# Row statistics for the next stage's normalisation, taken at the end of each stage

## The chip, the cores and the metric

The kernel runs on one core of one Trainium2 chip. The metric is the device time of one execution in microseconds. Three executions of the kernel before took 2994.44, 2995.75 and 3001.46 us, so the median is 2995.75 us.

## What is computed

The input `x` is 1024 tokens of 512 numbers. Two layers of blocks work on it. Each block normalises the rows (mean and variance over the 512 numbers of a token), computes something from the normalised rows and adds the result to `x`:

```python
def _layernorm(x, axis=-1, eps=1e-05):
    m = jnp.mean(x, axis=axis, keepdims=True)
    v = jnp.var(x, axis=axis, keepdims=True)
    return (x - m) / jnp.sqrt(v + eps)
# the pattern of every block: x = x + block(_layernorm(x))
```

The blocks, in the order in which the kernel runs them, are: attention with 32 heads of 16 (stage L0a), an expert choice of one in four with low-rank weights (L0f), attention with one head of 128 (L0b), the low-rank block again (L0g), attention with 32 heads of 128 (L1a), a routed block with 16 experts of which each token takes four (L1f), attention with heads of 16 again (L1b), and the routed block again (L1g).

## The kernel before

`x` stays in SBUF for the whole run, as `g.x`: eight tiles (`NT = 8`) of 128 tokens by 512 numbers in f32. The run is a row of stages: `constants` (it loads `x` and builds a few masks), the eight blocks above, and `store`. Every stage allocates its own semaphores and its own SBUF tiles, and ends with a barrier of all engines (line 73). No instruction of a stage, and none of its DMAs, is issued before the stage ahead of it has passed that barrier. So the loads of a stage's weights start when the stage starts.

Each engine works off its own list in order. Waits name a semaphore and a value.

At the start of each block stage VectorE (DVE) runs `ln_stats` (line 111): eight `bn_stats`, one for each tile of `x` (line 114), eight `bn_aggr` (line 117), one addition of the epsilon for all tiles (line 119), then a wait for ScalarE (ACT), which takes one square root for all tiles in `ln_root` (line 127), and a reciprocal (line 121). Then `ln_row` (line 133) writes the normalised tiles one by one, two ahead, and TensorE (PE) turns each by four transposes (`ln_turn`, line 141).

What stands between the first rows and the first products differs from stage to stage:

- `attention16` (L0a, L1b): DVE and PE wait for six loads (`w_loaded` at 96) after two rows.
- `lora_ffn` (L0f, L0g): PE turns one row, then waits for three loads (`loaded` at 48); DVE waits for the same three after two rows. The last of the three is `ebias`. The first product behind them is line 808.
- `single_head` (L0b): DVE waits for five loads (`loaded` at 80) straight behind the statistics and ahead of the first row, for line 1011; PE waits for the same five ahead of everything. The last one is `bo`.
- `attention128` (L1a): DVE waits for four loads (`loaded` at 64) after two rows, for line 1441. The last one is `bo`.
- `routed_ffn` (L1f, L1g): DVE waits for two small loads (`loaded` at 32) after two rows, for lines 1876 and 1878; the last one is `gb`. Then row 2 is written, and `xl` of row 0 (line 1059) starts a loop in which PE, ACT and DVE hand each row on.

Each stage ends with additions of the block's result into the tiles of `g.x` on DVE: line 740 (`attention16`), 855 (`lora_ffn`), 1028 (`single_head`), 1472 (`attention128`) and 2028 (`routed_ffn`, where both summands come back from HBM by DMA). In `attention128` the order of the last steps on DVE is written out by hand: the additions of the last head come in the order of tiles 0, 1, 3, 2, 4, 5, 6, 7, with work on the probabilities (line 1456, tile `pl`) between them, and PE's last large product waits for the last `pl`.

Of the kernel before, what the change touches and what calls it, by code (L numbers as in the profile page):

```python
# [14 lines left out]
P = 128  # L15
# [60 lines left out]
class Shared:  # L76


    def __init__(self, nc, ctx):
# [8 lines left out]
        self.sum_dram = [nc.dram_tensor(f"sum{i}", (T + P, H), F32, kind="Internal").ap() for i in range(3)]  # L88
        self.padded = nc.alloc_semaphore("padded")
# [8 lines left out]

class Normalisation:


    def __init__(self, sb, sem, depth=2):
        self.depth = depth
        self.xn = sb("xn", [P, depth, H])
        self.stats, self.mv = sb("stats", [P, NT, 6]), sb("mv", [P, NT, 2])
        self.veps, self.std, self.rstd = sb("veps", [P, NT]), sb("std", [P, NT]), sb("rstd", [P, NT])
        self.step, self.std_ready = sem("ln_step"), sem("std_ready")
        self.row_ready, self.turned = sem("row_ready"), sem("row_turned")


def ln_stats(dve, g, n):

    for t in range(NT):
        dve.bn_stats(n.stats[:, t, :], g.x[:, t, :]).then_inc(n.step, 1)
    for t in range(NT):
        dve.wait_ge(n.step, NT)
        dve.bn_aggr(n.mv[:, t, :], n.stats[:, t, :]).then_inc(n.step, 1)
    dve.wait_ge(n.step, 2 * NT)
    dve.tensor_scalar_add(n.veps[:, :], n.mv[:, :, 1], EPS).then_inc(n.step, 1)
    dve.wait_ge(n.std_ready, 1)  # L120
    dve.reciprocal(n.rstd[:, :], n.std[:, :]).then_inc(n.step, 1)
    dve.wait_ge(n.step, 2 * NT + 2)


def ln_root(act, n):
    act.wait_ge(n.step, 2 * NT + 1)
    act.activation(n.std[:, :], n.veps[:, :], ACT.Sqrt).then_inc(n.std_ready, 1)


def ln_row(dve, g, n, t):  # L130
    if t >= n.depth:
        dve.wait_ge(n.turned, t - n.depth + 1)
    dve.tensor_scalar(n.xn[:, t % n.depth, :], g.x[:, t, :], n.mv[:, t, 0:1], n.rstd[:, t:t + 1],
                      ALU.subtract, ALU.mult).then_inc(n.row_ready, 1)
# [23 lines left out]
def constants(nc, g, d):  # L158
    with stage(nc, "const") as (sb, sem):
        done = sem("done")  # L160
        loaded = sem("loaded")
        with nc.Block() as block:
            @block.sync
            def _(sp):
                sp.dma_start(g.x[:, :, :], d["x"]).then_inc(loaded, 16)
                sp.wait_ge(loaded, 16)

# [140 lines left out]
def attention16(nc, g, d, name, first):  # L308
    with stage(nc, name) as (sb, sem):
        ln = Normalisation(sb, sem)  # L310
# [3 lines left out]
        with nc.Block() as block:  # L314
# [69 lines left out]
            def _(act):  # L384
# [31 lines left out]
                ln_root(act, ln)  # L416
# [41 lines left out]

# [286 lines left out]
def lora_ffn(nc, g, d, name):  # L745

    with stage(nc, name) as (sb, sem):
        ln = Normalisation(sb, sem)
# [17 lines left out]
        with nc.Block() as block:  # L766
# [17 lines left out]
            def _(act):  # L784
                ln_root(act, ln)
                for t in range(NT + 2):
# [3 lines left out]
                    if t >= 2:  # L790
# [3 lines left out]
                        act.activation(zT[:, t % 2, :], g.bank(3)[:, 0:P], ACT.Copy).then_inc(zT_ready, 1)  # L794

# [32 lines left out]
            def _(dve):  # L828
                ln_stats(dve, g, ln)
                ln_row(dve, g, ln, 0)  # L830
                ln_row(dve, g, ln, 1)
                dve.wait_ge(filled, NE0 + 2)
                dve.wait_ge(loaded, 48)
                for t in range(NT + 2):
# [18 lines left out]
                    if t >= 2:  # L853
                        dve.wait_ge(out_ready, t - 1)
                        dve.tensor_tensor(g.x[:, t - 2, :], g.bank((t - 2) % 3), g.x[:, t - 2, :], ALU.add)\
                            .then_inc(added, 1)

def single_head(nc, g, d, name):  # L860
    with stage(nc, name) as (sb, sem):
        ln = Normalisation(sb, sem)
# [20 lines left out]
        with nc.Block() as block:  # L883
# [13 lines left out]
            def _(act):  # L897
                ln_root(act, ln)
# [36 lines left out]
                ctx_copy(NT - 1)  # L935

# [71 lines left out]
            def _(dve):  # L1008
                ln_stats(dve, g, ln)
                dve.wait_ge(loaded, 80)  # L1010
                dve.tensor_scalar(bqs[:, :], bq[:, 0:1], -SCALE, None, ALU.mult).then_inc(bias_ready, 1)
                for t in range(NT):
                    ln_row(dve, g, ln, t)
                for t in range(NT):
# [18 lines left out]
                for qt in range(NT):  # L1033
# [7 lines left out]
                    if qt >= 2:  # L1041
                        add(qt - 2)
                add(NT - 2)
                add(NT - 1)

# [108 lines left out]
ROPES = list(LIN)  # L1154

# [41 lines left out]
def attention128(nc, g, d, name):  # L1197
    with stage(nc, name) as (sb, sem):
        ln = Normalisation(sb, sem)
# [48 lines left out]
        with nc.Block() as block:  # L1248
# [44 lines left out]
            def _(act):  # L1293
                ln_root(act, ln)
# [3 lines left out]
                for s in ACT_STEPS:  # L1298
# [36 lines left out]
                    else:  # L1335
# [13 lines left out]
                        mm.then_inc(lin_ready, 1)  # L1349

# [85 lines left out]
            def _(dve):  # L1436
                ln_stats(dve, g, ln)
# [702 lines left out]
```

## Time and profile before

| | |
|---|---|
| median of three executions | 2995.75 us |
| the profiled execution, its own time | 2997.02 us |
| its span in the profile | 2995.0 us |
| PE busy | 2652.2 us, 89% of the span |
| DVE busy | 1907.5 us, 64% |
| ACT busy | 1514.3 us, 51% |
| POOL busy | 822.2 us, 27% |
| mean granted TensorE clock | 0.945 of 2.4 GHz |

The profile lists, engine by engine, each instruction with its line, the tile that it writes, the tiles that it reads, its start and its duration. A timeline line reads: start in us from the span's start, duration in us, engine, line, operation, out<-in, the shape, and how many instructions of that kind are merged into it. What stands in brackets is the time that the engine had been idle before it, and what ended that. Busy time is no proof of a bound: what bounds a stretch is read from which wait ended last there.

### The profile page before, as it was taken

Reading aid. Unit: us, or ns where it says so; the run is one execution under the profiler, and the core shown is the slowest. Engines: PE = TensorE matmul, PEld = TensorE weight load, DVE = VectorE, ACT = ScalarE, POOL = GpSimd, SP = SyncE. Lnnn points to the kernel's source line nnn. Section 1 sums busy time; section 2 is a strip of 40 time slices with the busy share of each in tenths; the row PEclk is TensorE's granted clock in tenths of the full one; section 3 lists DMA queues with packets and bytes.
Section 4 is the critical chain, followed back from the end, with each engine's and each line's share of the span. In section 5 each row is a group of like instructions: output and inputs, shape, how many; then the busy total and the mean of one; then the engine's idle time right before and its main releaser. Section 6 shows DMA issues by size and latency. Waiting matters only on the chain. (4 is left out here: it accounts for less than half of the span.)

```text
span 2995.0 us, 46427 instructions
## 1 busy us (share of the span) xinstructions
PE 2652.2 (89%) x14824; PEld 1793.2 (60%) x14886; DVE 1907.5 (64%) x3382; ACT 1514.3 (51%) x2540; POOL 822.2 (27%) x777
## 2 busy tenths in 40 slices
PE   6789988886999999999999987999578888778995
PEld 4444434454888888888888864666344444345663
DVE  5666642444777787777777766677556666166774
ACT  4466661222555555555555541566265666324663
POOL 1200000104343443445335301455120000003552
PEclk9799998997999999999999988999788999979998
DMA  2100000001000000000000023988500000029887
GB/s 76 71 1 0 0 1 16 19 17 46 19 22 22 22 22 18 22 22 26 15 22 25 8 92 135 297 201 199 144 1 1 0 0 0 11 107 322 211 201 197
DMA packets 68154, 196.92 MB, mean 66 GB/s; under 512 B 9040, under 2 KB 9936, under 8 KB 62608
## 3 DMA queue, kind: packets, MB, share of 16 engines
q1 hardware_dynamic: 46928, 145.44, 14.2%
q0 software_dynamic: 21056, 49.30, 8.7%
q8 instruction: 96, 1.57, 0.2%
q14 instruction: 74, 0.61, 0.1%
HBM read 154.33 MB, written 40.37 MB: 65 GB/s over the span
## 5 line engine op out<-in xcount | busy, mean ns | idle before, releaser
L1315 ACT ACTIVATE L1a_ph<-single 128x512 fp32r<-128x512 f32 (+3 forms) x384 | 174.2, 489 | 180.4 <-PE single L1402 179.7
L698 DVE TENSOR_REDUCE L1b_least<-single 128x1 f32<-128x512 f32 (+3 forms) x304 | 191.2, 660 | 107.9 <-PE single L520 75.9
L698 DVE TENSOR_REDUCE L0a_least<-single 128x1 f32<-128x512 f32 (+3 forms) x304 | 191.1, 660 | 106.9 <-PE single L520 75.5
L1456 DVE TENSOR_TENSOR L1a_pl<-single,L1a_ph 128x512 fp32r<-128x512 f32 (+3 forms) x384 | 199.5, 549 | 52.7 <-ACT L1a_ph L1315 52.0
L1472 DVE SCALAR_TENSOR_TENSOR x<-single,L1a_rinv,x 128x512 f32<-128x512 f32 x256 | 189.5, 745 | 58.4 <-PE single L1066 58.4
L1306 ACT ACTIVATE L1a_probs<-pair,L1a_least 128x128 f32<-128x128 f32 (+7 forms) x256 | 190.0, 744 | 72.0 <-DVE L1a_least L1450 70.8
L1450 DVE TENSOR_REDUCE L1a_least<-pair 128x1 f32<-128x128 f32 (+7 forms) x256 | 190.8, 750 | 43.3 <-PE pair L1391 42.6
L1283 POOL TENSOR_TENSOR L1a_swapped<-L1a_swapped,L1a_sin 128x512 f32<-128x512 f32 x80 | 129.8, 1622 | 303.7 <-ACT L1a_swapped L1347 303.7
L409 ACT ACTIVATE L1b_probsT<-pair 128x896 f32<-128x896 f32 (+2 forms) x192 | 151.2, 811 | 67.4 <-PE pair L539 48.1
L409 ACT ACTIVATE L0a_probsT<-pair 128x896 f32<-128x896 f32 (+2 forms) x192 | 151.2, 811 | 65.9 <-PE pair L539 46.5
L1402 PE MATMUL single<-ident,L1a_probs 128*128 128x128 f32 x1152 | 169.0, 274 | 1.4 <-ACT L1a_probs L1306 1.4
L1064 PE MATMUL single<-L1a_xh,L1a_wh 128*128 128x512 f32 x384 | 160.4, 418 | 6.0 <-POOL L1a_wl L1272 4.6
L1066 PE MATMUL single<-L1a_xh,L1a_wl 128*128 128x512 f32 x384 | 152.6, 397 | 0.0
L1065 PE MATMUL single<-L1a_xl,L1a_wh 128*128 128x512 f32 x384 | 152.6, 397 | 0.0
L1289 POOL TENSOR_TENSOR L1a_ql<-L1a_lin,L1a_qh 128x512 fp32r<-128x512 f32 x64 | 85.6, 1337 | 234.9 <-DVE L1a_qh L1494 234.9
L1888 DVE TENSOR_TENSOR L1g_wl<-L1g_store,L1g_wh 128x1024 fp32r<-128x1024 f32 x94 | 111.2, 1222 | 60.3 <-ACT L1g_wh L1704 59.2
L1888 DVE TENSOR_TENSOR L1f_wl<-L1f_store,L1f_wh 128x1024 fp32r<-128x1024 f32 x94 | 111.2, 1223 | 59.9 <-ACT L1f_wh L1704 58.9
L1064 PE MATMUL pair<-L1a_kh,L1a_qh 128*128 128x512 f32 (+3 forms) x384 | 141.0, 367 | 6.9 <-POOL L1a_ql L1289 5.5
L1402 PEld LDWEIGHTS single<-ident,L1a_probs 128*128 128x128 f32 x1152 | 130.0, 141 | 13.2 <-ACT L1a_probs L1306 1.7
L516 PE MATMUL single<-L1b_qkT 96*128 (+3 forms) x384 | 122.6, 356 | 13.0 <-DVE L1b_least L698 8.5
L1065 PE MATMUL pair<-L1a_kl,L1a_qh 128*128 128x512 f32 (+3 forms) x384 | 133.1, 347 | 0.0
L1066 PE MATMUL pair<-L1a_kh,L1a_ql 128*128 128x512 f32 (+3 forms) x384 | 133.1, 347 | 0.0
(517 smaller groups left out, 7052.1 us busy)
## 6 DMA issues: line engine op xcount, KB each, us to landing
L1f_wd<-in_L1f_w SPq DMA_DIRECT2D x48, 512.0 KB, 4.3
L1g_wd<-in_L1f_w SPq DMA_DIRECT2D x48, 512.0 KB, 4.2
L1a_raw<-in_L1a_w SPq DMA_DIRECT2D x80, 256.0 KB, 2.6
L1f_store<-in_L1f_w SPq DMA_DIRECT2D x16, 1024.0 KB, 7.9
L1g_store<-in_L1f_w SPq DMA_DIRECT2D x16, 1024.0 KB, 8.4
sum<-L0a_pad_row SPq DMA_DIRECT2D x2, 2304.0 KB, 11.7
sum<-x SPq DMA_DIRECT2D x16, 256.0 KB, 2.9
x<-sum SPq DMA_DIRECT2D x16, 256.0 KB, 4.7
```

What stands on the lines that cost most here:

```text
L409: act.activation(a.probsT[:, i % 2, j, 0:n], g.pair[u % 2][:, 0:n], ACT.Exp, scale=-1.0)\
L698: dve.tensor_reduce(a.least[:, part, qt, first:first + heads], g.bank(4 + f % 2)[:, 0:heads * w].rearrange("p (j k) -> p j k", j=heads), A ...
L1064: pe.matmul(out, wh, xh, start=start, stop=False)
L1065: pe.matmul(out, wh, xl, start=False, stop=False)
L1066: return pe.matmul(out, wl, xh, start=False, stop=stop)
L1306: act.activation(probs[:, u % 2, 0:n], g.pair[u % 2][:, 0:n], ACT.Exp, bias=least[:, u % 4:u % 4 + 1], scale=-1.0, accum_out=rsum[:, h % 2 ...
L1315: act.activation(p_tile(ph, u, i), turned_bank(u, i), ACT.Copy).then_inc(p_high, 1)
L1402: mm = pe.transpose(g.bank(4 + b % 2)[:, k * P:(k + 1) * P], probs[:, u % 2, kt * P:(kt + 1) * P], g.ident[:, :])
L1450: dve.tensor_reduce(least[:, u % 4:u % 4 + 1], g.pair[u % 2][:, 0:(u % NT + 1) * P], AX_X, ALU.min)\
L1456: dve.tensor_tensor(p_tile(pl, u, i), turned_bank(u, i), p_tile(ph, u, i).bitcast(F32), ALU.subtract)\
L1472: dve.scalar_tensor_tensor(out=g.x[:, t, :], in0=aux_bank(("O", h, t)), scalar=rinv[:, h % 2, t:t + 1], in1=g.x[:, t, :], op0=ALU.mult, op ...
L1888: dve.tensor_tensor(wl[:, s, :, :], src, wh[:, s, :, :].bitcast(F32), ALU.subtract).then_inc(w_split, 1)
```

## The change

Each stage now takes the statistics of the stage behind it, and no stage but `constants` takes its own. Two sets of small tiles (`Moments`) live for the whole run, and each stage swaps them.

- For each tile of `x`, `ln_next` waits for the addition into that tile (or, in `constants`, for the load of `x`), then issues three instructions on DVE, each waiting for the one before: `bn_stats`, `bn_aggr`, and the addition of the epsilon for this tile alone. A call for a tile stands behind the addition into the next tile; the calls for the last two tiles stand behind the last addition (in `single_head` the last three calls are spread over the last two additions).
- ACT takes the square root of the first seven tiles in one instruction (`ln_next_root`) when their values are there; DVE takes one reciprocal of them at the very end (`ln_next_scale`).
- The next stage has only the eighth tile's root (`ln_last_root`, ACT, at its start) and reciprocal (`ln_last_scale`, DVE, behind the first two rows) left; `ln_row` of the eighth tile waits for it.
- `ln_stats` and its calls at the start of the eight block stages are gone. The last block stage, L1g, takes no statistics for a stage behind it.
- Each stage has two more semaphores.

```diff
-def ln_stats(dve, g, n):
-
-    for t in range(NT):
-        dve.bn_stats(n.stats[:, t, :], g.x[:, t, :]).then_inc(n.step, 1)
-    for t in range(NT):
-        dve.wait_ge(n.step, NT)
-        dve.bn_aggr(n.mv[:, t, :], n.stats[:, t, :]).then_inc(n.step, 1)
-    dve.wait_ge(n.step, 2 * NT)
-    dve.tensor_scalar_add(n.veps[:, :], n.mv[:, :, 1], EPS).then_inc(n.step, 1)
...
+LATE = NT - 1
+LAST = "L1g"
+
+
+def ln_last_root(act, n):
+
+    act.activation(n.now.std[:, LATE:NT], n.now.veps[:, LATE:NT], ACT.Sqrt).then_inc(n.std_ready, 1)
+
+
+def ln_last_scale(dve, n):
+
     dve.wait_ge(n.std_ready, 1)
...
+    dve.reciprocal(n.now.rstd[:, LATE:NT], n.now.std[:, LATE:NT]).then_inc(n.step, 1)
+
+
+def ln_next(dve, g, n, t, added, count, turn=None):
+
+    m, turn = n.after, t if turn is None else turn
+    dve.wait_ge(added, count)
+    dve.bn_stats(m.stats[:, t, :], g.x[:, t, :]).then_inc(n.next_step, 1)
+    dve.wait_ge(n.next_step, 3 * turn + 1)
+    dve.bn_aggr(m.mv[:, t, :], m.stats[:, t, :]).then_inc(n.next_step, 1)
+    dve.wait_ge(n.next_step, 3 * turn + 2)
+    dve.tensor_scalar_add(m.veps[:, t:t + 1], m.mv[:, t, 1:2], EPS).then_inc(n.next_step, 1)
+
+
+def ln_next_root(act, n):
+
+    act.wait_ge(n.next_step, 3 * LATE)
+    act.activation(n.after.std[:, 0:LATE], n.after.veps[:, 0:LATE], ACT.Sqrt).then_inc(n.next_std_ready, 1)
+
+
+def ln_next_scale(dve, n):
+
+    dve.wait_ge(n.next_std_ready, 1)
+    dve.reciprocal(n.after.rstd[:, 0:LATE], n.after.std[:, 0:LATE]).then_inc(n.next_step, 1)
...
+            @block.vector
+            def _(dve):
+                for t in range(NT):
+                    ln_next(dve, g, ln, t, loaded, 16)
+                ln_next_scale(dve, ln)
...
             @block.vector
             def _(dve):
-                ln_stats(dve, g, ln)
                 ln_row(dve, g, ln, 0)
                 ln_row(dve, g, ln, 1)
+                ln_last_scale(dve, ln)
                 dve.wait_ge(a.w_loaded, 96)
...
                     dve.tensor_tensor(g.x[:, t, :], g.bank(t % 2), g.x[:, t, :], ALU.add).then_inc(a.added, 1)
+                    if t >= 1:
+                        ln_next(dve, g, ln, t - 1, a.added, t)
+                ln_next(dve, g, ln, NT - 1, a.added, NT)
+                ln_next_scale(dve, ln)
...
+                        turn = LAST_ADDED.index(t) if h == HEADS128 - 1 else 0
+                        if turn >= 1:
+                            before = LAST_ADDED[turn - 1]
+                            ln_next(dve, g, ln, before, added, ADDED["o", h, before], turn - 1)
...
                     dve.wait_ge(back_loaded[t], 32)
                     dve.tensor_tensor(g.x[:, t, :], other[:, t, :], g.x[:, t, :], ALU.add).then_inc(back, 1)
+                    if name != LAST and t >= 1:
+                        ln_next(dve, g, ln, t - 1, back, t)
+                if name != LAST:
+                    ln_next(dve, g, ln, NT - 1, back, NT)
+                    ln_next_scale(dve, ln)
```

## Rows read from the trace of the kernel before

**Rows 1.** Timeline, from the end of L0a to L0f's first product.

```profile
484.94 0.69 DVE L740 TENSOR_TENSOR x<-pair,x 128x512 f32<-128x512 f32 x1 [3.75 <-PE pair L624]
...
486.55 1.28 ACT L127 ACT_TABLE_LOAD   x1 [5.41 <-PEq L73]
486.59 4.84 DVE L114 BATCH_NORM_STATS2 L0f_stats<-x 128x6 f32<-128x512 f32 x8 [0.96 <-PEq L73]
...
487.42 0.42 SPq L771 DMA_DIRECT2D L0f_ebias<-in_L0f_bias  x1
...
491.47 0.64 DVE L117 BATCH_NORM_AGGREGATE L0f_mv<-L0f_stats 128x2 f32<-128x6 f32 x8
...
492.83 1.00 DVE L133 TENSOR_SCALAR L0f_xn<-x,L0f_mv,L0f_rstd 128x512 f32<-128x512 f32 x2
493.43 1.97 PE L141 MATMUL single<-ident,L0f_xn 128*128 128x128 f32 x8 [8.53 <-DVE L0f_xn L133]
...
495.23 1.93 PE L808 MATMUL single<-L0f_ga,L0f_xT 128*128 128x36 f32 x8
```

**Rows 2.** Tiles x and L0f_mv: count, ns min/median/max, first and last start, shape.

```profile
L114 DVE BATCH_NORM_STATS2 L0f_stats<-x x8: 675/676/695, 486.6 to 490.8; 128x6 f32<-128x512 f32 x8
...
L117 DVE BATCH_NORM_AGGREGATE L0f_mv<-L0f_stats x8: 147/148/182, 491.5 to 492.0; 128x2 f32<-128x6 f32 x8
...
L119 DVE TENSOR_SCALAR L0f_veps<-L0f_mv x1: 172/172/172, 492.1 to 492.1; 128x8 f32<-128x8 f32 x1
```

**Rows 3.** DMA issues: transfer, queue, count, KB each, us from issue to landing.

```profile
L0b_bo<-in_L0b_bo SPq DMA_DIRECT2D x1, 256.0 KB, 4.5
...
L0f_ebias<-in_L0f_bias SPq DMA_DIRECT2D x1, 2.0 KB, 4.8
...
L0g_ebias<-in_L0f_bias SPq DMA_DIRECT2D x1, 2.0 KB, 5.4
L1f_gb<-in_L1f_bias SPq DMA_DIRECT2D x1, 8.0 KB, 2.7
```

**Rows 4.** Timeline, what the starts of L0a, L0b and L1a wait for.

```profile
21.34 6.89 PE L468 MATMUL pair<-L0a_w,L0a_xT 128*128 128x512 f32 x16 [3.23 <-DMA L0a_bd<-in_L0a_bd]
...
548.52 0.43 SPq L890 DMA_DIRECT2D L0b_bo<-in_L0b_bo  x1
...
553.10 0.15 DVE L1011 TENSOR_SCALAR L0b_bqs<-L0b_bq 128x1 f32<-128x1 f32 x1
...
700.39 0.18 DVE L1441 TENSOR_SCALAR L1a_bias<-L1a_bias 128x32 f32<-128x32 f32 x1 [0.39 <-DMA L1a_bo<-in_L1a_bo]
```

**Rows 5.** Timeline, the start of L1f (L1g repeats it).

```profile
1766.38 0.43 SPq L1596 DMA_DIRECT2D L1f_gb<-in_L1f_bias  x1
...
1773.20 0.18 DVE L1876 CAST L1f_gwh<-L1f_gw 128x64 fp32r<-128x64 f32 x1
...
1774.66 0.69 DVE L1059 TENSOR_TENSOR L1f_xl<-single,L1f_xh 128x512 fp32r<-128x512 f32 x1 [0.56 <-ACT L1f_xh L1052]
```

**Rows 6.** Timeline, DVE in the middle of L0b.

```profile
610.19 1.23 DVE L1020 TENSOR_REDUCE L0b_least<-pair 128x1 f32<-128x1024 f32 x1 [0.91 <-PE pair L964]
```

**Rows 7.** Timeline, DVE at the end of L1a.

```profile
1753.04 1.29 DVE L1456 TENSOR_TENSOR L1a_pl<-single,L1a_ph 128x512 fp32r<-128x512 f32 x2 [0.41 <-ACT L1a_ph L1315]
...
1761.75 1.44 DVE L1472 SCALAR_TENSOR_TENSOR x<-single,L1a_rinv,x 128x512 f32<-128x512 f32 x2 [1.14 <-PE single L1066]
...
1763.64 1.45 DVE L1472 SCALAR_TENSOR_TENSOR x<-single,L1a_rinv,x 128x512 f32<-128x512 f32 x2 [0.45 <-PE single L1066]
```

**Rows 8.** Timeline, the second and the last of L1f's eight closing additions.

```profile
2124.16 0.69 DVE L2028 TENSOR_TENSOR x<-L1f_store,x 128x512 f32<-128x512 f32 x1 [1.36 <-DMA L1f_store<-sum]
...
2132.32 0.69 DVE L2028 TENSOR_TENSOR x<-L1f_store,x 128x512 f32<-128x512 f32 x1 [0.59 <-DMA L1f_store<-sum]
```

**Rows 9.** Stretches: us, busy PE PEld DVE ACT POOL, PEclk, DMA share, GB/s.

```profile
488.00:489.00 1.00, 0.00 (x0) 0.00 (x0) 1.00 (x3) 0.00 (x0) 0.00 (x0) 0.76 0.98 166
...
502.00:503.00 1.00, 1.00 (x3) 0.33 (x2) 0.00 (x0) 0.00 (x0) 0.00 (x0) 0.91 0.00 0
```

More of the change, by code:

```diff
@@ L88, in __init__ @@
         self.sum_dram = [nc.dram_tensor(f"sum{i}", (T + P, H), F32, kind="Internal").ap() for i in range(3)]
+        self.moments = tuple(Moments(sb, n) for n in range(2))
         self.padded = nc.alloc_semaphore("padded")
@@ L95, in bank, with __init__ @@
         return self.pair[i // 2][:, (i % 2) * HALF:(i % 2 + 1) * HALF] if i < 4 else self.single[i - 4][:, :]
+class Moments:
+    def __init__(self, sb, n):
+        self.stats, self.mv = sb(f"stats{n}", [P, NT, 6]), sb(f"mv{n}", [P, NT, 2])
+        self.veps, self.std, self.rstd = sb(f"veps{n}", [P, NT]), sb(f"std{n}", [P, NT]), sb(f"rstd{n}", [P, NT])
 class Normalisation:
-    def __init__(self, sb, sem, depth=2):
+    def __init__(self, sb, sem, g, depth=2):
         self.depth = depth
         self.xn = sb("xn", [P, depth, H])
-        self.stats, self.mv = sb("stats", [P, NT, 6]), sb("mv", [P, NT, 2])
-        self.veps, self.std, self.rstd = sb("veps", [P, NT]), sb("std", [P, NT]), sb("rstd", [P, NT])
+        self.now, self.after = g.moments
+        g.moments = (self.after, self.now)
@@ L132, in ln_row @@
         dve.wait_ge(n.turned, t - n.depth + 1)
-    dve.tensor_scalar(n.xn[:, t % n.depth, :], g.x[:, t, :], n.mv[:, t, 0:1], n.rstd[:, t:t + 1],
+    if t == LATE:
+        dve.wait_ge(n.step, 1)
+    dve.tensor_scalar(n.xn[:, t % n.depth, :], g.x[:, t, :], n.now.mv[:, t, 0:1], n.now.rstd[:, t:t + 1],
                       ALU.subtract, ALU.mult).then_inc(n.row_ready, 1)
@@ L856, in _ @@
                             .then_inc(added, 1)
+                    if t >= 3:
+                        ln_next(dve, g, ln, t - 3, added, t - 2)
+                ln_next(dve, g, ln, NT - 1, added, NT)
+                ln_next_scale(dve, ln)
 def single_head(nc, g, d, name):
     with stage(nc, name) as (sb, sem):
-        ln = Normalisation(sb, sem)
+        ln = Normalisation(sb, sem, g)
         xT = sb("xT", [P, KC, T])
@@ L935, in _ @@
                 ctx_copy(NT - 1)
+                ln_next_root(act, ln)
             @block.tensor
@@ L1013, in _ @@
                     ln_row(dve, g, ln, t)
+                    if t == 1:
+                        ln_last_scale(dve, ln)
                 for t in range(NT):
@@ L1042, in _ @@
                         add(qt - 2)
+                    if qt >= 3:
+                        ln_next(dve, g, ln, qt - 3, added, qt - 2)
                 add(NT - 2)
+                ln_next(dve, g, ln, NT - 3, added, NT - 2)
                 add(NT - 1)
+                ln_next(dve, g, ln, NT - 2, added, NT - 1)
+                ln_next(dve, g, ln, NT - 1, added, NT)
+                ln_next_scale(dve, ln)
 def turned_rows_high(act, g, ln, xh, ready):
@@ L1154 @@
 ROPES = list(LIN)
+LAST_ADDED = [s[2] for s in DVE_STEPS if s[0] == "o" and s[1] == HEADS128 - 1]
 def piece_of(step):
@@ L1494, in _ @@
                         dve.tensor_copy(rope_to(kind, of, half, kh, qh), lin[:, r, :]).then_inc(rot_high, 1)
+                ln_next(dve, g, ln, LATE, added, ADDED["o", HEADS128 - 1, LATE])
+                ln_next_scale(dve, ln)
 GU = KC
```

41 lines of the change are left out of this document (23 added, 18 removed).

## The prediction

> **What bounds the kernel now.** I read the timeline around each of the eight stage boundaries, since the change moves work only there, and asked at each which wait ended last. At the end of L0a the last addition starts at 484.94, the barrier lets L0f go at 486.55, DVE takes its statistics, and the first normalised row starts at 492.83 [rows 1]. So 6.24 us lie between the first `bn_stats` (486.59) and the first row, and PE is idle all that time. This is what the change goes for: eight stages times 6.24 is 49.9 us.
>
> The second view is that of the DMA issues: a stage's loads are issued when the stage starts, and some land later than the statistics end. Then the removed time was not on the path. The third is the end of each stage, where the new work goes: is DVE waiting between its additions, or is it the last to finish?
>
> **The price of one tile.** `bn_stats` lasts 0.676 us alone, `bn_aggr` 0.148, the addition of epsilon 0.172 [rows 2]. Each waits for the one before. Such a hand-over took 0.04 us: eight `bn_stats` from 486.59 last 4.84 and end at 491.43, and `bn_aggr` starts at 491.47 [rows 1]. The next instruction, where it does not depend on the last one, starts some 0.08 us before its end: eight times 0.676 would be 5.41, and they took 4.84 [rows 1, 2]. A tile therefore costs 0.676 + 0.04 + 0.148 + 0.04 + 0.172 - 0.08 = 1.0 us on DVE. Before, a tile cost 4.84/8 + 0.64/8 = 0.69, as the small instructions followed each other without waits. Bounds: 0.96 (a 0.04 hand-over is hidden) and 1.12 (no overlap at the end, and one hand-over more).
>
> The Trainium skill (VectorE: DVE Perf Modes, The DRAIN you can't avoid) says that the next operation doesn't start until the pipeline is empty, and that the semaphore costs nothing extra. The 4.84 us above contradict the first half. By the page a tile would cost 1.08 to 1.12, and the sum below would be some 3 us higher.
>
> **What is added at the stage ends.** A call of `ln_next` keeps back whatever stands behind it on DVE.
>
> - Simple tail (L0a, L0f, L0b, L0g, L1b): the earlier tiles lie in DVE's idle time between additions, 3.75 us a tile in L0a [rows 1]. In `lora_ffn` they delay the choice of an expert for the next tile by about 0.6 us, with PE's main product as cover. In L0b the tightest place is the minimum at line 1020, ahead of which DVE idles 0.91 us for PE [rows 6]; 1.0 us goes in there, so 0.1 us could show, and I take nothing. If the cover were gone, each of these tiles would cost its 1.0. Behind the last addition stand two tiles and the reciprocal of about 0.2: 2.2 us, five times, 11.0 us. The barrier then follows as before (485.63 to 486.55, [rows 1]).
> - `constants`: eight tiles and the reciprocal behind the load of `x`, and nothing to hide them: 8 x 1.0 + 0.2 = 8.2 us. The weights of L0a are issued only behind the barrier, so they are late by the same.
> - L1a, ahead of PE's last large product: two tiles come before the last `pl` (line 1456), ahead of which DVE idled 0.41 us [rows 7]. 2.0 - 0.4 = 1.6 us. Bounds 0 (other idle time absorbs it) and 2.0.
> - L1a, behind it: four additions and now five tiles. The additions ran from 1761.75 to 1763.64 + 1.45 = 1765.09 [rows 7]. After: 4 x 0.70 + 5 x 1.0 + 0.2 = 8.0, that is to 1769.75. Cost 4.7 us. PE's last two products wait for additions in this queue, but DVE is later than they are anyway.
> - L1f: the closing additions follow the loads, one each 1.36 us, the last seven from 2124.16 to 2132.32 + 0.69 = 2133.01 [rows 8]. With a tile of 1.0 behind each addition of 0.61, DVE needs 1.6 a tile and becomes the bound: 7 x 0.61 + 8 x 1.0 + 0.2 = 12.5, to 2136.6. Cost 3.6 us. L1g takes no statistics: 0.
>
> Sum of costs: 11.0 + 8.2 + 1.6 + 4.7 + 3.6 = 29.1 us. The square root of seven tiles runs on ACT beside the last tile's statistics. That of the eighth, at the stage start, and its reciprocal are needed six rows later. Two more semaphores a stage I take at nothing; the bound above is 0.1 us a stage.
>
> **What is gained at the stage starts.** Times stay those of the old trace, with the stage start held fixed.
>
> - L0a: PE had been idle 3.23 us when the last of six loads landed and let the products start at 21.34 [rows 4]. Gain 0. L1b repeats this (12.3 us from its start to the load): 0.
> - L0b: `bo` is issued at 548.52 and lands 4.5 us later, at 553.02 [rows 3, 4]. DVE's first instruction behind it starts at 553.10 [rows 4], and it stands ahead of the rows. Statistics and load end together: gain at most 0.1. I take 0.
> - L1a: DVE waits for `bo` until 700.39, after 0.39 us of idling [rows 4]. Only the first two rows get earlier. Gain 0.
> - L0f: `ebias` is issued at 487.42 and lands at 492.22 [rows 1, 3]. PE has then to turn row 1, four of the eight transposes that took 1.97 us [rows 1], some 0.9 us, and starts line 808 at 493.2. Before: 495.23 [rows 1]. Gain 2.1, bounds 1.1 and 3.0 (two turnings or none).
> - L0g: the same, but `ebias` lands 0.6 us later [rows 3]: gain 1.5.
> - L1f: `gb` lands at 1766.38 + 2.7 = 1769.08 [rows 3, 5]. Lines 1876 and 1878 and row 2 then took from 1773.20 to 1774.10, where DVE began to wait for ACT [rows 5]: 0.9 us. So line 1059 starts at 1770.0 instead of 1774.66 [rows 5]. Gain 4.6. What follows is a chain of hand-overs that moves as a whole. L1g: `gb` lands 0.2 later in its stage, gain 4.5.
>
> Sum of gains: 2.1 + 1.5 + 4.6 + 4.5 = 12.7 us. Net: 29.1 - 12.7 = 16.4 us slower. The profiled execution took 2997.02 us (span 2995.0 and 2.0 around it), so it would take 3013.4; the median of the runs is 1.3 us lower, which gives 3012.1 us, 0.55% more. A measurement of this kernel can tell about 0.3% (9 us) from no change.
>
> **Rivals.**
>
> - The loads get out of the way (faster). If the loads land earlier once DVE no longer reads `x` while they write, stages held by loads gain too. With no stage held by its loads the gain is 49.9 - 29.1 = 20.8 us: 2975 us. It turns the sign once the loads land some 2 us earlier in each of the eight stages. For it: loads and statistics do overlap, with the DMA engines busy for 0.98 of the stretch from 488 to 489 [rows 9]. Against it: in L0a DVE had nothing to do for the last microseconds, and the loads still landed 3.23 us after PE had run dry [rows 4]. Chance 0.04.
> - The clock stays up (no change). The granted clock fell between 488 and 489, some 3.6 us after PE's last product, and rose between 502 and 503 [rows 9], 8.7 us after PE's first transposes at 493.43 [rows 1]. At half speed that loses at most 4.3 us. If the shorter pause held the clock at 2.4 GHz in L0f, L0g, L1f and L1g, up to 17 us would come back: 2995 us. Against it: PE's first transpose would start at 485.63 + 2.2 + 0.92 + 0.64 = 489.4, still behind the fall, and PE then stops again for the load. Chance 0.05. The Trainium skill (TensorE: Matmul & The Clock Gate, Why this matters for your kernels) advises to avoid pauses of PE for this reason; by it shorter pauses speak for this change, and by it the time would be this rival's 2995.
> - Dearer hand-overs (slower still). Some 32 tiles lie on the path (8 + 10 + 7 + 8, less what idle time covers). If a tile costs 1.5 us instead of 1.0, that adds 16 us: 3028 us. Against it: the 0.04 us measured. Chance 0.05.
> - The square root comes late. At the ends of five stages (L0a, L0b, L1a, L1f, L1b) ACT changes its table; L0f and L0g have it already. If the 1.28 us of the load [rows 1] started only when the seventh tile's values are there, root and load take 1.5 against the 1.0 of the last tile: 0.5 us each, 3015 us in all, within the range. Against it: the load at 486.55 ran ahead of its wait [rows 1]. Chance 0.06. The Trainium skill (ScalarE: Activation LUTs, What ACT_TABLE_LOAD costs) puts a switch at 2.66 us, with a drain; by that it would be some 1.9 us a stage, near 3020.
>
> **How the numbers follow.** The forecast of 3012 us has a chance of 0.80. Its own range: the price of a tile moves it by -1 to +4, the middle of L1a by -1.6 to +0.4, the starts of L0f and L0g by 1 each way, the moment at which the clock rises after each boundary by some 3 in all (L0f's 8.7 us is one draw), the median of three runs by 2. Together that is 3006 to 3018, and with the late root and part of the clock's rival 3005 to 3019. Faster by over 0.3%: 0.04. Within 0.3%: 0.10, from the clock and from the case that several tails are half hidden. Slower by over 0.3%: 0.86.
>
> **What would show it.** In the new profile: L0a's products start some 8 us later than 21.34. From the last addition's end to the next stage's first instruction it is 3.1 us in the simple tails against 0.9. L0b's line 1011 and L1a's line 1441 stand as far from their stage's start as before, with some 6 to 8 us of idle DVE ahead. L1f's line 1059 starts 4.6 us nearer to its stage's start. The closing additions of L1f come 1.6 us apart. The prediction is wrong if the loads of L0b, L1a, L0a or L1b land earlier in their stages, or if a tile costs much other than 1.0 us.

## The result, and the profile after

The changed kernel took 3011.77 us, the median of 13 executions (3008.34 to 3016.97). Beside them 13 executions of the kernel before had a median of 3001.46 us (2993.57 to 3005.6). The ratio is 1.0041, with a 95% interval of 1.003 to 1.0053: slower by 12.3 us, 9 to 16 (the ratio on record is not that of the two medians, which are 10.3 us apart). A second comparison, told below, gave 1.0049 (1.003 to 1.0067). So the change costs about 0.4 to 0.5%.

| | before | after |
|---|---|---|
| profiled execution | 2997.02 us | 3011.77 us |
| its span | 2995.0 us | 3009.7 us |
| PE busy | 2652.2 us | 2660.0 us |
| DVE busy | 1907.5 us | 1923.2 us |
| mean granted clock | 0.945 | 0.946 |

What follows are timelines of the changed kernel, in the columns told with the profile of before. A call of the new `ln_next` is three lines: L140 (`bn_stats`), L142 (`bn_aggr`), L144 (epsilon). The first and the last call of `constants`, with the reciprocal, and PE's first products in L0a (they answer to the first line of [rows 4]):

```profile
8.64 0.69 DVE L140 BATCH_NORM_STATS2 stats<-x 128x6 f32<-128x512 f32 x1 [8.64 <-DMA x<-in_x]
9.37 0.18 DVE L142 BATCH_NORM_AGGREGATE mv<-stats 128x2 f32<-128x6 f32 x1
9.59 0.15 DVE L144 TENSOR_SCALAR veps<-mv 128x1 f32<-128x1 f32 x1
...
15.69 0.68 DVE L140 BATCH_NORM_STATS2 stats<-x 128x6 f32<-128x512 f32 x1
...
16.69 0.19 DVE L156 RECIPROCAL rstd<-std 128x7 f32<-128x7 f32 x1
```

```profile
29.65 1.22 PE L510 MATMUL pair<-L0a_w,L0a_xT 128*128 128x512 f32 x1 [7.82 <-DMA L0a_bd<-in_L0a_bd]
```

Eight calls take from 8.64 to 16.69, so 1.006 us each. The products start 8.31 us later than at 21.34, and PE idles 7.82 us for the same load `bd` where it idled 3.23: the shorter start only makes the wait for the load longer.

DVE from L0a's last addition to L0f's first row, and PE to L0f's first product (they answer to [rows 1]):

```profile
495.98 0.69 DVE L782 TENSOR_TENSOR x<-pair,x 128x512 f32<-128x512 f32 x1 [2.75 <-PE pair L666]
496.59 0.68 DVE L140 BATCH_NORM_STATS2 stats<-x 128x6 f32<-128x512 f32 x1
...
497.59 0.68 DVE L140 BATCH_NORM_STATS2 stats<-x 128x6 f32<-128x512 f32 x1
...
498.60 0.19 DVE L156 RECIPROCAL rstd<-std 128x7 f32<-128x7 f32 x1
499.77 0.76 DVE L164 TENSOR_SCALAR L0f_xn<-x,mv,rstd 128x512 f32<-128x512 f32 x1 [0.98 <-PEq L73]
```

```profile
505.41 1.11 PE L172 MATMUL single<-ident,L0f_xn 128*128 128x128 f32 x4 [3.71 <-DMA L0f_ebias<-in_L0f_bias]
506.31 0.91 PE L855 MATMUL single<-L0f_ga,L0f_xT 128*128 128x36 f32 x4
```

Two calls and the reciprocal stand behind the last addition. From its start to the first row it is 3.79 us, of which 2.14 are new. From that row to line 855 it is 6.54 us, and PE waits 3.71 of them for `ebias`. From the last addition to the first product it was 10.29 us before and is 10.33 now: tail and gain cancel.

Where L0b and L1a begin, DVE waits for `bo` (the last two lines of [rows 4]):

```profile
566.65 0.15 DVE L1062 TENSOR_SCALAR L0b_bqs<-L0b_bq 128x1 f32<-128x1 f32 x1 [7.37 <-DMA L0b_bo<-in_L0b_bo]
...
716.67 0.18 DVE L1502 TENSOR_SCALAR L1a_bias<-L1a_bias 128x32 f32<-128x32 f32 x1 [8.14 <-DMA L1a_bo<-in_L1a_bo]
```

The end of L1a on DVE (it answers to [rows 7]). First the second of the last head's eight additions before, the one into tile 1:

```profile
1750.16 0.75 DVE L1472 SCALAR_TENSOR_TENSOR x<-single,L1a_rinv,x 128x512 f32<-128x512 f32 x1 [0.39 <-PE single L1066]
```

The same after, from the second of the last head's eight additions to L1f's first `xl` (the last line of [rows 5]):

```profile
1764.94 0.75 DVE L1533 SCALAR_TENSOR_TENSOR x<-single,L1a_rinv,x 128x512 f32<-128x512 f32 x1 [0.38 <-PE single L1125]
1765.61 0.68 DVE L140 BATCH_NORM_STATS2 stats<-x 128x6 f32<-128x512 f32 x1
...
1769.34 1.28 DVE L1517 TENSOR_TENSOR L1a_pl<-single,L1a_ph 128x512 fp32r<-128x512 f32 x2
...
1778.98 0.69 DVE L1525 TENSOR_TENSOR L1a_cl<-single,L1a_ch 128x512 fp32r<-128x512 f32 x1 [6.62 <-ACT L1a_ch L1381]
1780.82 0.75 DVE L1533 SCALAR_TENSOR_TENSOR x<-single,L1a_rinv,x 128x512 f32<-128x512 f32 x1 [1.15 <-PE single L1125]
...
1785.86 0.75 DVE L1533 SCALAR_TENSOR_TENSOR x<-single,L1a_rinv,x 128x512 f32<-128x512 f32 x1
...
1788.54 0.19 DVE L156 RECIPROCAL rstd<-std 128x7 f32<-128x7 f32 x1
...
1793.66 0.68 DVE L1118 TENSOR_TENSOR L1f_xl<-single,L1f_xh 128x512 fp32r<-128x512 f32 x1
```

From the addition at 1764.94 to the one behind PE's last large product (1780.82) it is 15.88 us. The same two additions stood 11.59 apart before (1750.16 and 1761.75). The two calls account for 1.5 of that; the rest is new and I had no term for it. The granted clock shows what it is. Stretches at the end of L1a (columns as in [rows 9]):

```profile
1765.00:1769.00 4.00, 2.62 (x14) 1.49 (x12) 3.93 (x8) 1.82 (x4) 0.00 (x0) 1.00 0.00 0
1769.00:1770.00 1.00, 0.00 (x0) 0.00 (x0) 0.93 (x5) 0.19 (x1) 0.00 (x0) 0.91 0.00 0
1770.00:1771.00 1.00, 0.28 (x1) 0.31 (x2) 1.00 (x3) 0.00 (x0) 0.00 (x0) 0.50 0.00 0
1771.00:1775.00 4.00, 4.00 (x10) 3.13 (x10) 1.30 (x5) 0.00 (x0) 0.00 (x0) 0.50 0.00 0
```

PE ahead of its last large product, before (first line) and after (the two behind it); "issue" stands where the last wait was for the last `pl`, which ends 0.10 us earlier:

```profile
1754.43 0.47 PE L1064 MATMUL single<-L1a_ph,L1a_vh 128*128 128x512 f32 x1 [1.62 <-issue]
```

```profile
1767.44 1.06 PE L1463 MATMUL single<-ident,L1a_probs 128*128 128x128 f32 x8 [0.72 <-DVE L1a_pl L1517]
...
1770.72 0.77 PE L1123 MATMUL single<-L1a_ph,L1a_vh 128*128 128x512 f32 x1 [2.22 <-issue]
```

PE idled here before too, for 1.62 us, and the clock stayed up. Now it idles 0.72 us ahead of the last transposes of the probabilities and 2.22 us behind them. Near the end of the microsecond from 1769 to 1770, in the longer of the two gaps, the clock falls to 1.2 GHz, and the last large product runs at it until between 1776 and 1777. It takes 7.6 us where it took 4.8.

L1f's last closing additions follow each other in 1.61 us, where they had been 1.29 to 1.36 apart (the last two of eight, with the first instruction of the call between; they answer to [rows 8]):

```profile
2151.48 0.68 DVE L2097 TENSOR_TENSOR x<-L1f_store,x 128x512 f32<-128x512 f32 x1
2152.08 0.69 DVE L140 BATCH_NORM_STATS2 stats<-x 128x6 f32<-128x512 f32 x1
...
2153.09 0.68 DVE L2097 TENSOR_TENSOR x<-L1f_store,x 128x512 f32<-128x512 f32 x1
```

The first three additions still wait for their loads (the third 0.51 us); the last five don't, and DVE sets the pace.

### The profile page after: what moved, and what is told of

Read it like the earlier page. It is cut to its first block and busy times, and to the rows that moved or that the text cites. A ratio compares the mean times of both kernels' runs of the same rounds, so it can differ in the third digit from the quotient of the medians.

```text
span 3009.7 us, 46566 instructions
## 1 busy us (share of the span) xinstructions
PE 2660.0 (88%) x14886; PEld 1788.7 (59%) x14886; DVE 1923.2 (64%) x3446; ACT 1517.6 (50%) x2548; POOL 824.0 (27%) x777
## 5 line engine op out<-in xcount | busy, mean ns | idle before, releaser
L1125 PE MATMUL single<-L1a_ph,L1a_vl 128*128 128x512 f32 (+3 forms) x384 | 133.6, 348 | 0.0
L1123 PE MATMUL single<-L1a_ph,L1a_vh 128*128 128x512 f32 (+3 forms) x384 | 131.5, 343 | 2.2 <-issue 2.2
L1124 PE MATMUL single<-L1a_pl,L1a_vh 128*128 128x512 f32 (+3 forms) x384 | 133.5, 348 | 0.0
```

The lines of the kernel that those rows point to most:

```text
L1123: pe.matmul(out, wh, xh, start=start, stop=False)
L1124: pe.matmul(out, wh, xl, start=False, stop=False)
L1125: return pe.matmul(out, wl, xh, start=False, stop=stop)
```

## The experiments

Each was timed against the kernel before on the same chip in five rounds. For each I give two numbers, both against the kernel before. The first is the time by the ratio of the runs (times 2997 us), with its interval. The second is the sum from the trace: what the touched places took longer or shorter in the profile. These are the eight ways from one stage's last addition to the first product or instruction behind the loads of the next, and, inside two stages, the way from L1a's addition into tile 1 to its last addition, and L1f's eight closing additions. It leaves out how long the rest of each stage took, which varies by 5 to 9 us from profile to profile in each of the five long stages (attention with heads of 16 took 461 to 468 us from first product to last addition). That calls between the additions of the simple tails cost nothing is read from the additions themselves. From the first to the last of the eight it is 31.13 us in L0a, 31.48 in L0f, 27.49 in L0b, 31.48 in L0g and 31.13 in L1b before, and within 0.02 us of that in all eleven other profiles, with and without calls between them.

| version | by the runs, us | sum from the trace, us | of it, fall of the clock in L1a |
|---|---|---|---|
| changed | +12.3 (9.0 to 15.9) | +19.0 | 2.8 |
| changed, again | +14.7 (9.0 to 20.1) | +18.5 | 2.7 |
| ends and starts | +25.5 (19.5 to 31.2) | +31.2 | 2.7 |
| L0a own, eight calls elsewhere | +9.6 (6.0 to 12.9) | +19.2 | 2.9 |
| L0a own | +5.1 (1.2 to 8.7) | +7.2 | 0 |
| L1a's calls moved | +9.0 (5.1 to 12.9) | +12.5 | 0 |
| without the ends | -12.0 (-15.9 to -7.8) | -4.8 | 0 |
| without the ends, again | -12.0 (-16.8 to -7.2) | -5.0 | 0 |
| early for two stages | -9.0 (-13.2 to -4.8) | -6.4 | 0 |
| early for four stages | -12.0 (-16.8 to -7.5) | -10.6 | 0 |
| before, on held statistics | +0.3 (-3.6 to 4.5) | +0.1 | 0 |

The two columns order the versions alike, except for the one with eight calls elsewhere and those without the ends (the two rows of the changed kernel are one version). The runs are 1 to 10 us below the traces in all rows but the last. In four rows (changed, eight calls elsewhere, and both without the ends) the sum from the trace lies outside the interval of the runs. I come back to this at the end.

**Without the ends.** The calls at the ends of the seven block stages go; the later stages use the statistics of the first.

```diff
-                    if t >= 1:
-                        ln_next(dve, g, ln, t - 1, a.added, t)
-                ln_next(dve, g, ln, NT - 1, a.added, NT)
-                ln_next_scale(dve, ln)
```

(and so in each stage, with `ln_next_root`)

> The changed kernel without its statistics at the end of the seven block stages: every stage uses the statistics that the first stage, the one that loads x, took (so the values of the later stages are normalised with stale statistics; nothing else of the work is left out). This leaves the shorter starts (gains) and the 8.2 us of the first stage (a cost). My theory, that the starts win 12.7 us because loads hold most of them, expects 8.2 - 12.7 = 4.5 us below the kernel before, about 2995 us, and 21 to 24 us below the changed kernel (20.9 us of calls, and 2.8 us if the slower clock in L1a's last product comes from the calls ahead of it). Start to first product: L0a, L0b, L1a, L1b as long as in the changed kernel, with the idle time ended by the loads bd, bo, bo. The rival, that the loads would come earlier if the end of the stage ahead did not disturb them, expects the starts to win over 30 us and a time below 2980 us.

The trace gives what my theory has, -4.8 us: +8.43 in the first stage, L0f -2.09, L0g -1.86, L1f -4.66, L1g -4.72, L0b and L1b 0, L1a +0.5. The gains are 13.3 us where I had 12.7, and the starts of L0a, L0b, L1a and L1b gain nothing. DVE at the start of L0b in this version:

```profile
552.87 0.69 DVE L897 TENSOR_TENSOR x<-pair,x 128x512 f32<-128x512 f32 x1 [0.91 <-PE pair L861]
560.67 0.15 DVE L1052 TENSOR_SCALAR L0b_bqs<-L0b_bq 128x1 f32<-128x1 f32 x1 [7.11 <-DMA L0b_bo<-in_L0b_bo]
```

It is 7.80 us from addition to line 1052, and was 7.85 before. The rival that loads get out of the way is false. Against the changed kernel the trace has 23.7 us less and the runs 24, where 21 to 24 were expected. But against the kernel before the runs say -12 us (ratio 0.996, 0.9947 to 0.9974). The next two versions are about that.

**The kernel before, on held statistics.** Every instruction of before stays; only the numbers by which the rows are normalised are those of L0a.

```diff
-    dve.tensor_scalar(n.xn[:, t % n.depth, :], g.x[:, t, :], n.mv[:, t, 0:1], n.rstd[:, t:t + 1],
+    dve.tensor_scalar(n.xn[:, t % n.depth, :], g.x[:, t, :], g.held[0][:, t, 0:1], g.held[1][:, t:t + 1],
```

> The kernel before, with all its instructions, but each stage normalises with the means and roots that L0a took (two small copies in L0a keep them; every stage still takes its own statistics and doesn't use them). The work is the same and only the numbers differ. It tells what the version without statistics at the ends owes to its numbers: that one took some 10 us less than the kernel before where its trace shows 4.5 us less between the stages. If the numbers set the clock, this kernel shows a mean granted clock near 0.950 where the kernel before shows 0.946, and takes 5 to 8 us less than it. If they don't, it takes the same time within 2 us, and the starts must have won more than my theory says.

Ratio 1.0001 (0.9988 to 1.0015), mean clock 0.946 over its twelve executions. So the numbers don't account for 7 us. The profiled execution alone has 0.950: the mean clock of one profile says little.

**Without the ends, again.** The same kernel as the first.

> The changed kernel without its statistics at the ends, once more. The first time it took 10.6 us less than the kernel before by the mean of its runs, where its trace shows 4.5 us less between the stages, and the numbers it works on were excluded as the cause. If that was a draw of the clock, this run gives some 4.5 us; if it stays near 10 us with a mean granted clock near 0.950, the removal of the ends has an effect on the clock that the sum of the terms has no line for.

Ratio 0.996 (0.9944 to 0.9976), -12 us again, with a mean clock of 0.949 against 0.945 beside it, and -5.0 us by the trace. The sum from the touched places is steady: the two profiled executions took 2995.16 us (the slowest of its twelve) and 2983.44, and their sums differ by 0.3. So it was no single draw: some 7 us come from the rest of the stages, where one profile can't show a place for them. This stays open.

**L1a's calls behind the last `pl`.**

```diff
-                        if turn >= 1:
-                            before = LAST_ADDED[turn - 1]
-                            ln_next(dve, g, ln, before, added, ADDED["o", h, before], turn - 1)
+                        for k in {3: (0, 1, 2, 3), 5: (4,), 6: (5,), 7: (6,)}.get(turn, ()):
+                            before = LAST_ADDED[k]
+                            ln_next(dve, g, ln, before, added, ADDED["o", h, before], k)
```

> The changed kernel with one thing moved: in L1a the calls for tiles 0, 1, 3 and 2 stand behind the addition into tile 2, that is behind the last work on the probabilities, where DVE idled 6.6 us beside the last large product. My theory, that the calls between the steps on the probabilities delay that product by 1.5 us and that the sparse work of TensorE there lets the clock fall, expects the product to start 1.5 us earlier relative to the addition into tile 1, to run at its full clock (4.8 us, not 7.6), and the tail behind the last addition to fall by 0 to 1.0 us: 4.3 to 5.3 us below the changed kernel. The rival, that the clock's fall comes from what ran long before and not from these calls, expects the product to take 7.6 us still, and 1.5 to 2.5 us.

The end of L1a on DVE, and the same stretches:

```profile
1761.23 0.75 DVE L1533 SCALAR_TENSOR_TENSOR x<-single,L1a_rinv,x 128x512 f32<-128x512 f32 x1 [0.41 <-PE single L1125]
...
1771.03 0.69 DVE L1525 TENSOR_TENSOR L1a_cl<-single,L1a_ch 128x512 fp32r<-128x512 f32 x1 [0.86 <-ACT L1a_ch L1381]
1772.86 1.44 DVE L1533 SCALAR_TENSOR_TENSOR x<-single,L1a_rinv,x 128x512 f32<-128x512 f32 x2 [1.14 <-PE single L1125]
```

```profile
1764.00:1765.00 1.00, 0.00 (x0) 0.00 (x0) 0.89 (x2) 0.57 (x2) 0.00 (x0) 1.00 0.00 0
1765.00:1771.00 6.00, 4.86 (x24) 4.12 (x24) 4.89 (x15) 0.60 (x1) 0.00 (x0) 1.00 0.00 0
```

The two additions are 11.63 us apart again (11.59 before), the clock stays at 2.4 GHz, the product takes 4.9 us, and of DVE's 6.62 us of idling 0.86 are left: four calls are free there. The last four additions now go from 1772.86 to 1776.92, 4.06 us instead of 5.04. In all that is 5.2 us (4.25 and 0.98), as expected. By the runs it is +9.0 us against +12.3 of the changed kernel, and the two intervals overlap, so the traces carry this and not the times.

**L0a takes its own, `constants` none.**

```diff
-                for t in range(NT):
-                    ln_next(dve, g, ln, t, loaded, 16)
-                ln_next_scale(dve, ln)
...
+                if first:
+                    ln_own(dve, g, ln)
                 ln_row(dve, g, ln, 0)
```

> The changed kernel, but the first stage takes no statistics, and L0a takes its own at its start as in the kernel before. My theory, that L0a's first product waits for the load bd that starts with the stage, so that the statistics of x are free there and cost their full length in the first stage, expects 8.3 us below the changed kernel, with the first product of L0a at 21.3 us instead of 29.7 us. The rival, that statistics in the first stage are partly beside something and L0a's start is shortened, expects 0 to 3 us.

PE's first products:

```profile
21.49 2.93 PE L523 MATMUL pair<-L0a_w,L0a_xT 128*128 128x512 f32 x3 [3.22 <-DMA L0a_bd<-in_L0a_bd]
```

21.49 instead of 29.65: 8.2 us, where 8.3 was expected and the rival had 0 to 3. By the runs this version takes 7 us less than the changed kernel. In this profile the clock did not fall at the end of L1a, though the calls stand there as in the changed kernel and PE idles just as long (0.73 and 2.21 us). A microsecond in the longer gap, and the one behind it:

```profile
1758.00:1759.00 1.00, 0.00 (x0) 0.00 (x0) 0.96 (x4) 0.00 (x0) 0.00 (x0) 1.00 0.00 0
1759.00:1760.00 1.00, 0.48 (x2) 0.47 (x3) 1.00 (x3) 0.00 (x0) 0.00 (x0) 1.00 0.00 0
```

The two additions are 13.12 us apart here: 1.53 for the calls, and no fall.

**Eight calls more at the end of L0g.** The last version, with L1a brought as late as in the changed kernel by work elsewhere.

```diff
                 ln_next_scale(dve, ln)
+                if name == "L0g":
+                    for t in range(NT):
+                        dve.bn_stats(m.stats[:, t, :], g.x[:, t, :]).then_inc(ln.next_step, 1)
...
```

> The version in which L0a takes its own statistics, with eight more calls of three instructions (on tiles that nothing reads) at the end of L0g. It brings L1a as late as in the changed kernel (8.0 us), but by another stage. In both profiles of the changed kernel the clock was at half in L1a's last large product, and in the one of the version without these 8 us it was not. If what decides is when L1a begins, the product takes 7.6 us again. If it is chance, or the statistics in the first stage themselves, it takes 4.8 us. Either way eight calls behind each other cost 8.0 us, so 8.0 us above the version for L0a (10.8 us with the fall).

```profile
1767.00:1768.00 1.00, 0.00 (x0) 0.00 (x0) 0.96 (x4) 0.05 (x1) 0.00 (x0) 0.97 0.00 0
1768.00:1769.00 1.00, 0.42 (x1) 0.45 (x2) 1.00 (x2) 0.00 (x0) 0.00 (x0) 0.50 0.00 0
1769.00:1775.00 6.00, 6.00 (x16) 4.66 (x16) 1.15 (x5) 0.00 (x0) 0.00 (x0) 0.52 0.00 0
```

The clock falls again, and the additions are 16.0 us apart. The eight calls lengthen the way from L0g's last addition to L1a's line 1441 by 8.5 us. By the runs this version is at +9.6 us, 4.5 above the last one where the trace says 12.0: its row has the largest gap between the two columns. If most executions don't have the fall, it is 2.9 us smaller, and no more. The profiled execution was the slowest of the twelve (3018.39 us, median 3010.95).

**The changed kernel, again.**

> The changed kernel once more, for its time beside the same runs of the kernel before, and a second profile. Its clock fell to half in L1a's last large product in the first profile. My theory of the calls between the steps on the probabilities says that they leave TensorE so little to do that it can fall, but that whether it does hangs on when the fall's moment comes: the product takes 4.8 or 7.6 us in this profile. The sum of the terms is 16 us above the kernel before, with the fall; 13.5 us without it.

The fall is there, with 15.8 us between the two additions. The sums in the expectation are 3 us too low: 16 is the sum of the terms without the fall. With it the trace has 18.5, and 19.0 in the first profile. By the ratio (+14.7) the runs stand nearer to the sum without it; the two medians are 18.05 us apart. With 6 runs this comparison can't tell the two.

**Ends and starts.** The changed kernel, and all statistics once more at each start.

```diff
+                ln_own(dve, g, ln)
                 ln_row(dve, g, ln, 0)
                 ln_row(dve, g, ln, 1)
-                ln_last_scale(dve, ln)
```

> The changed kernel with both: the statistics at the end of each stage, and all of them again at the start of each stage (those at the end are thrown away). This keeps the costs and takes the gains away. My theory expects the costs alone: 29.1 us above the kernel before (11.0 of five tails, 8.2 in the first stage, 6.3 in L1a, 3.6 behind L1f), 31.9 us if the clock falls again in L1a's last product; so 12.7 us above the changed kernel, all of it at the starts of L0f (2.1), L0g (1.6), L1f (4.7) and L1g (4.7). If a start were hidden in another way than by its loads, L0b, L1a or L1b would be longer too, up to 6 us each.

The trace has +31.2 us, expected were 31.9 with the fall, and the fall is there. The runs have +25.5. Against the changed kernel the starts are longer by 2.1 (L0f), 1.5 (L0g), 4.7 (L1f) and 4.7 us (L1g), and those of L0b, L1a, L1b and L0a are no longer (up to 0.6 shorter): 12.2 in the sums where 12.7 was expected.

**Only where a start is led.** Last, a kernel by the sum's own terms. Each call stands directly behind its addition, and tile 7 is left to the next stage; L1f gets tiles 0, 1, 3 and 2 only, all four behind the addition into tile 2; and the four stages that wait for loads take their own. The lines are shown against the changed kernel.

```diff
+TAKEN = {"L0f": 7, "L0g": 7, "L1f": 4, "L1g": 7}
...
-                    if t >= 1:
-                        ln_next(dve, g, ln, t - 1, a.added, t)
-                ln_next(dve, g, ln, NT - 1, a.added, NT)
+                    ln_next(dve, g, ln, t, a.added, t + 1)
                 ln_next_scale(dve, ln)
```

> Early statistics only where the traces show a start that they lead: for L0f, L0g and L1g of tiles 0 to 6, each directly behind its addition, where DVE idles up to 2.75 us before the next; for L1f of tiles 0, 1, 3 and 2 only, behind the addition into tile 2, beside the last large product. The tiles that are left (7; for L1f 4 to 7) are taken in the next stage behind its first two rows, where DVE waits for a load. L0a, L0b, L1a and L1b take all of their own at the start, as in the kernel before. My theory, that costs lie in tails and gains in starts and that the two add up, expects from the last addition to the first product, against the kernel before: L0f -1.9, L0g -1.6, L1f -2.5, L1g -4.5 us, nothing elsewhere, so about 10.5 us faster than the kernel before (some 2986 us). The rival, that instructions added to the idle times of DVE delay its additions all the same (one call is 1.0 us), expects 0.5 to 1.0 us more in each of the four stages that take them, and 6 to 8 us.

> The same, for L1f and L1g alone: the other six stages take all of their own statistics at their start. My theory expects 7.0 us below the kernel before, and 3.5 us above the version for four stages. If the gains at L0f and L0g, whose first product waits for the load ebias, are none, the two versions take the same time.

The version for four stages had a median of 2986.21 us against 2996.39 of the kernel before beside it: ratio 0.996 (0.9944 to 0.9975), 12 us faster (7 to 17). The one for two: 0.997 (0.9956 to 0.9984), 9 us faster. The traces have -10.6 and -6.4, where 10.5 and 7.0 were expected. The first is made of L0f -1.96, L0g -1.88, L1f -3.09 and L1g -3.97. DVE from L1b's last addition to L1g's first `xl` in the first of them:

```profile
2602.59 0.69 DVE L791 TENSOR_TENSOR x<-pair,x 128x512 f32<-128x512 f32 x1 [2.62 <-PE pair L675]
2603.20 0.19 DVE L153 RECIPROCAL rstd<-std 128x7 f32<-128x7 f32 x1
2604.53 1.11 DVE L184 TENSOR_SCALAR L1g_xn<-x,mv,rstd 128x512 f32<-128x512 f32 x2 [1.14 <-PEq L73]
2605.56 0.68 DVE L161 BATCH_NORM_STATS2 stats<-x 128x6 f32<-128x512 f32 x1
...
2607.89 0.16 DVE L168 RECIPROCAL rstd<-std 128x1 f32<-128x1 f32 x1 [1.25 <-ACT std L176]
...
2608.91 0.69 DVE L1125 TENSOR_TENSOR L1g_xl<-single,L1g_xh 128x512 fp32r<-128x512 f32 x1
```

6.32 us, where it was 10.29. Behind the addition only the reciprocal is left. The rival that calls in idle time delay the additions is false: in L0a, L0b, L1a and L1b the way from the first to the last of the eight additions is what it was before, to 0.04 us. Of L1g's 4.5 us half a microsecond is missing: DVE waits 1.25 us for the root of tile 7, which stands behind two copies on ACT. The two versions differ by 4.2 us in the traces, and their intervals overlap.

## Why the prediction was right

The forecast of slower and the range held, and so did the sum, place by place. That 3011.77 stands so near to 3012 is luck: the kernel before had 3001.46 in this comparison, not 2995.75. What was forecast is +16.4 us. The ratio says +12.3 (9.0 to 15.9), so that 16.4 lies just above its interval, and the second one +14.7 (9 to 20). Two things that the forecast didn't have pull against each other: a fall of the clock that adds 2.8 us in the trace, and an unexplained gap by which the runs stay below the traces.

The terms, each read from the two profiles of before and after as the difference of two starts, so that drift inside a stage doesn't enter:

| term | forecast | trace |
|---|---|---|
| a tile | 1.0 | 1.006 |
| `constants`, to L0a's first product | 8.2 | 8.31 |
| five simple tails | 11.0 | 10.65 (2.11 to 2.16 each) |
| L1a, ahead of the last product | 1.6 | 1.51 |
| L1a, behind it | 4.7 | 4.59 |
| L1f's end, eight additions and what follows | 3.6 | 3.69 |
| starts of L0f, L0g | -2.1, -1.5 | -2.10, -1.56 |
| starts of L1f, L1g | -4.6, -4.5 | -4.67, -4.72 |
| starts of L0a, L0b, L1a, L1b | 0 | +0.5 in all |
| sum, without the fall of the clock | 16.4 | 16.2 |

What carried it: reading at each start which wait ends last, and then asking whether the load or the statistics would be the later one without the statistics. The four starts that I put at nothing are at nothing, within 0.6 us, in every version.

- The price of a tile. `bn_aggr` took 0.18 us alone, not the 0.148 of eight in a row [rows 2], and the epsilon for one number 0.15, not 0.172; the two errors cancel. The next `bn_stats` starts 0.08 us before the epsilon's end, as forecast, so a full drain between all instructions, by which a tile would cost 1.08 to 1.12, is not borne out. The Trainium skill (VectorE: DVE Perf Modes, The DRAIN you can't avoid) says more than the prediction took from it: that a next operation which is not held starts earlier. The 0.08 us agree with that.
- L0b's 0.1 us can't be told from one profile: from the first instruction behind the loads to the last addition L0b took 76.67 us, and 77.67 before, and 76.7 to 78.1 over all twelve. Its additions kept their distances (27.49 us).
- L1f's end is partly luck. The forecast counted from the second addition; counted so, the trace has 4.2 us. The first gap was 0.5 us shorter than before, which brings the whole to 3.7. Over the six profiles with calls behind all of these additions the whole is 3.7 to 4.2 us.
- The late root was false. ACT loaded its table at 492.21, ahead of its wait, and the root of seven tiles ran at 497.71, beside the last tile. DVE idles ahead of the reciprocal (L156) in no stage. Nor is a table load dearer than 1.28 us here: at 2651.39 one began 0.02 us behind the activation ahead of it, and the next activation began at 2652.68, 1.29 us later.
- The clock did not stay up either. At L0f's start PE's pause fell from 8.53 us to 4.64, and the granted clock, 1.00 from 499 to 500, was 0.54 from 500 to 501 and 0.50 behind that. It was at half around the starts of L0g, L1f and L1g too, as long as before in the first two and 3.4 us less in L1g. So the rival's 17 us did not come back.
- The clock was the part that I missed. I looked for it only at the starts, as a gain. It cost 2.8 us at the end of L1a. The step that fell short is the one that priced the two calls ahead of the last `pl` by DVE's time alone: they also make PE idle 0.72 and 2.22 us within four microseconds, where it idled 1.62. Four of the five profiles with these calls have the fall; none of the seven without them has it, though PE idles 1.62 us in each. So, as far as twelve profiles tell, it takes the calls. That it also hangs on the moment is less sure: bringing L1a 8 us forward took the fall away in one profile, and putting the 8 us in elsewhere brought it back. One profile without the fall can't be told from chance.
- Open: the runs are below the sums from the traces in ten of eleven rows of the table, by 1 to 10 us, in four of them by more than the noise of the runs. The forecast was made as such a sum; the changed kernel's sum is 19.0 with the fall and 16.2 without, and the runs have 12.3. The fall in L1a, if most executions don't have it, accounts for 3 us in four of the rows, and for nothing in the others. The numbers that the kernel works on are excluded. The mean clock of the runs differs in the version without ends (0.950 and 0.949 against 0.946 and 0.945), which names the resource and not the reason. In one stage the traces show how the rest of a stage varies: L0a, from its first product to its last addition, took 461.1 to 462.3 us at a mean granted clock of 0.956, 463.0 to 463.2 at 0.952, 463.6 to 463.8 at 0.949 and 465.4 to 466.3 at 0.945, whatever the version. Why an execution gets one or the other is not shown.

## What to carry to other kernels

Work moved from the start of a stage to its end is a gain only where the start is led by that work and the end has idle time for it: look up both, stage by stage, and move it only there. A start that waits for a load gives nothing back, however much is taken out of it, and is itself idle time in which left-over work is free. Price an insertion on one engine by the gap that it opens on the others too: where PE's gaps grow, the clock may fall for the product behind them.

## What the runs showed of the hardware

- A normalised row of 128x512 (0.54 us, two in 1.00) took far longer beside POOL. At L0a's start, with POOL clearing a buffer from 18.02 to 20.38, two rows took 3.01 us, and the second ended right behind that instruction. `bn_stats` beside such work took its 0.68 as ever. The Trainium skill (SBUF — State Buffer, SBUF: two separate sides) says that VectorE in a two-port mode and GpSimd hold a pair of ports exclusively and the other blocks. The trace fits that: the second row began 0.1 us after the clearing began and ended 0.3 us after its end. No run here shows the mode or the ports. Here it cost nothing, since the load came later.

```profile
17.65 3.01 DVE L164 TENSOR_SCALAR L0a_xn<-x,mv,rstd 128x512 f32<-128x512 f32 x2 [0.77 <-PEq L73]
```

```profile
18.02 2.36 POOL L380 MEMSET L0a_stack<- 128x2560 bf16 x1
```

- The clock fell in PE's gap of 2.2 us at the end of L1a in four profiles of three versions (additions 15.8 to 16.0 us apart). It did not in an equal gap of another (13.12 apart), with the same instructions around it and L1a's start 8 us earlier, nor in the gap of 1.62 us in the seven profiles without the two calls.
